# Cross attention with layer norm on one core: the key sums are moved into the attention visit, and five smaller moves

## What is computed

```python
q = (x @ Wq.T + bq), k = (ctx @ Wk.T + bk), v = (ctx @ Wv.T + bv)     # split into 16 heads of 32
att = softmax(q @ k.T / sqrt(32))                                     # over the 750 keys
out = x + ((att @ v) @ Wo.T + bo)
out = (out - mean) / sqrt(var + 1e-5) * gamma + beta                  # over the 512 features
```

## Time and profile before

| | |
|---|---|
| median of 3 runs | 644.46 us (643.81 to 645.33) |
| the profiled execution | 644.03 us, of which the span of the instructions is 642.0 us |
| granted TensorE clock, mean | 0.996 |
| busy: TensorE, VectorE, ScalarE, GpSimd | 617.8, 480.1, 350.5, 453.5 us |

### The profile page before, as it was taken

The page is one execution under the profiler, slowest core; times in us unless marked ns, Lnnn a source line. Parts: engine busy times, 40 slices in busy tenths (PEclk is TensorE's granted clock), DMA queues, the critical chain, the costliest instruction groups (busy, mean ns, idle before and its releaser), DMA issues.

```text
span 642.0 us, 13640 instructions
## 1 busy us (share of the span) xinstructions
PE 617.8 (96%) x5217; PEld 422.1 (66%) x5217; DVE 480.1 (75%) x680; ACT 350.5 (55%) x673; POOL 453.5 (71%) x443
## 2 busy tenths in 40 slices
PE   9989999999999999999999999999999999999994
PEld 7756676766666667766666666666677666665542
DVE  4677677777887688776887678876888788765895
ACT  4524566565565456564665655654565656443661
POOL 9401686975878588785879858785887878866853
PEclk9999999999999999999999999999999999999998
DMA  9367633663256613754137631566136431330011
GB/s 298 127 180 166 148 85 73 125 149 67 63 112 140 147 42 89 162 138 107 28 87 162 146 77 47 128 148 143 35 89 165 99 66 40 96 91 21 2 50 37
DMA packets 96016, 67.02 MB, mean 104 GB/s; under 512 B 69892, under 2 KB 82192, under 8 KB 95952
## 3 DMA queue, kind: packets, MB, share of 16 engines
q1 hardware_dynamic: 95952, 66.16, 41.9%
HBM read 24.52 MB, written 3.67 MB: 44 GB/s over the span
## 4 chain that ended last, share of the span: by engine, by line
PE 81%; DVE 15%; issue 2%; ACT 1%; POOL 0%; POOLq 0%; DVEq 0%
PE ps_task L595 36%; PE ps_task L646 11%; PE ps_scores L606 11%; PE ps_scoresT L630 10%; DVE top L912 6%; PE ps_task L554 4%; PE ps_task L672 2%; PE ps_scores L595 2%; DVE attn_sums L919 2%; DVE attn_parts L934 2%; DVE y L881 1%; DVE stats L884 1%; DVE parts L869 1%; PE ps_scores L574 1%; PE ps_scores L658 1%
## 5 line engine op out<-in xcount | busy, mean ns | idle before, releaser
L793 ACT ACTIVATE probsT<-ps_scoresT 125x448 f32<-125x448 f32 x384 | 203.8, 545 | 200.6 <-PE ps_scoresT L630 198.9
L912 DVE TENSOR_REDUCE top<-ps_scores 112x1 f32<-112x750 f32 x256 | 235.4, 927 | 78.8 <-PE ps_scores L606 77.8
L1020 POOL TENSOR_TENSOR pair_sums<-probsT 125x672 f32<-125x672 f32 x122 | 198.5, 1627 | 111.0 <-ACT probsT L793 101.8
L630 PE MATMUL ps_scoresT<-stacks 100*125 100x224 f16 x768 | 134.8, 260 | 1.7 <-ACT probsT L793 1.1
L595 PE MATMUL ps_task<-wvT,ctxT 128*125 128x512 f16 x564 | 134.9, 379 | 0.9 <-DVE parts L869 0.9
L595 PE MATMUL ps_task<-ctxT,wkT 128*128 128x375 f16 x708 | 130.7, 323 | 0.1
L606 PE MATMUL ps_scores<-stacks 96*112 96x512 f16 (+1 forms) x512 | 126.2, 328 | 2.5 <-DVE top L912 2.5
L630 PEld LDWEIGHTS ps_scoresT<-stacks 100*125 100x125 f16 x768 | 93.6, 137 | 40.9 <-ACT probsT L793 6.4
L1025 POOL TENSOR_TENSOR head_sums<-pair_sums 125x224 f32<-125x224 f32 x122 | 88.8, 728 | 11.4
L595 PEld LDWEIGHTS ps_task<-wvT,ctxT 128*125 128x125 f16 x564 | 73.2, 136 | 33.7 <-DVE parts L869 1.1
L1028 POOL TENSOR_TENSOR head_sums<-head_sums,pair_sums 125x224 f32<-125x224 f32 x122 | 87.1, 714 | 9.6
(11 more groups left out here) (100 smaller groups left out, 524.1 us busy)
## 6 DMA issues: line engine op xcount, KB each, us to landing
stacks<-parts SPq DMA_DIRECT2D x256, 60.9 KB, 2.0
ctx_in<-in_ctx SPq DMA_DIRECT2D x8, 768.0 KB, 5.6
stacks<-parts SPq DMA_DIRECT2D x128, 46.9 KB, 2.0
resid<-in_x SPq DMA_DIRECT2D x8, 448.0 KB, 4.2
ctx_in<-in_ctx SPq DMA_DIRECT2D x7, 512.0 KB
out_y<-y SPq DMA_DIRECT2D x16, 224.0 KB, 2.4
x_in<-in_x SPq DMA_DIRECT2D x8, 256.0 KB, 3.1
stacks<-parts SPq DMA_DIRECT2D x128, 14.0 KB, 1.8
```

Of the source, the lines that this page charges most:

```text
L630: last = nc.tensor.matmul(ps_scoresT[0:KP, piece % 2, NQ * i:NQ * i + NQ], stacks[:, g, h, KP * k:KP * k + KP], stacks[:, g, h, Qc], start ...
L793: nc.scalar.activation(probsT[0:KP, g % 2, h, 2 * j:2 * j + 2, :].rearrange("p k q -> p (k q)"), ps_scoresT[0:KP, piece % 2, 0:2 * NQ], AC ...
L912: nc.vector.tensor_reduce(top[0:QP, g % 2, HG * q + h:HG * q + h + 1], ps_scores[0:QP, s % RING, 0:NK], AX.X, ALU.max).then_inc(top_ready, 1)
L1020: nc.gpsimd.tensor_tensor(pair_sums[0:KP], probsT[0:KP, g % 2, h, 0:3, :], probsT[0:KP, g % 2, h, 3:6, :], ALU.add).then_inc(pair_sums_rea ...
```

## The change

- `sum_keys` goes into step 1, right behind `attend`; `copy_attn` goes from step 3 to step 2. The steps of the inversion and all that follows stay.
- The pair sums of each unit's fourth head (h = 3, `FOURTH`) are made on VectorE (`add_fourth`, one addition of three tiles to three, 125 by 672) in step 0 of the unit, behind `save_task`; GpSimd waits for them and does the other two additions. The buffer `pair_sums` stays one for both engines, so `add_fourth` waits until GpSimd has finished the third head.
- The tasks ("V", 4) and ("Q", 3) change places (steps 7 and 8). ("V", 2) goes from step 28 to 24, ("Q", 0) from 24 to 26, ("Q", 1) from 26 to 28.
- `rstd_of` on GpSimd goes from steps 20 and 22 to 21 and 23, `times_gamma` on VectorE from 26 and 29 to 24 and 25, `plus_beta` on GpSimd from 27 and 30 to 24 and 26.
- ("V", 2) and the last three tiles of Wo leave the prologue; iteration 0 does them in steps 1, 9, 18 and 20. The load of Wo is split in halves; the second goes into `y`.
- The first `fill_stack(1)` is issued by GpSimd; `load_ctx(1, 0)` is issued before the first `fill_stack(0)`.

```diff
+    WO_HALF = DT // 2
-    OWN = {0: ("K", 2, 1), 2: ("Q", 2), 4: ("K", 3, 1), 5: ("V", 3), 7: ("V", 4), 8: ("Q", 3), 10: ("V", 5)}
-    NEXT = {12: ("K", 0, 0), 13: ("K", 1, 0), 15: ("V", 0), 16: ("V", 1), 21: ("K", 0, 1), 23: ("K", 1, 1), 24: ("Q", 0),
-            26: ("Q", 1), 28: ("V", 2), 29: ("K", 2, 0), 31: ("K", 3, 0)}
+    OWN = {0: ("K", 2, 1), 2: ("Q", 2), 4: ("K", 3, 1), 5: ("V", 3), 7: ("Q", 3), 8: ("V", 4), 10: ("V", 5)}
+    NEXT = {12: ("K", 0, 0), 13: ("K", 1, 0), 15: ("V", 0), 16: ("V", 1), 21: ("K", 0, 1), 23: ("K", 1, 1), 24: ("V", 2),
+            26: ("Q", 0), 28: ("Q", 1), 29: ("K", 2, 0), 31: ("K", 3, 0)}
+    FIRST = {1: ("V", 2), 9: ("W", "o", 1), 18: ("W", "o", 2), 20: ("W", "o", 3)}
-    SUMS_BEHIND = 2
-    STAGES = {**{("attend", k): (2, VISIT) for k in range(KT)}, "sum_keys": (2, SUMS_BEHIND), "copy": (2, 3), ("invert", 0): (2, 4),
+    STAGES = {**{("attend", k): (2, VISIT) for k in range(KT)}, "sum_keys": (2, VISIT), "copy": (2, 2), ("invert", 0): (2, 4),
               ("invert", 1): (2, 4), "scale": (2, 5), "high": (2, 6), "low": (2, 7)}
+    FOURTH = HG - 1
-    GAMMA_STEPS = (3 * UNIT + 2, 3 * UNIT + 5)
+    RSTD_STEPS = (2 * UNIT + 5, 2 * UNIT + 7)
+    GAMMA_STEPS = (3 * UNIT, 3 * UNIT + 1)
+    BETA_STEPS = (3 * UNIT, 3 * UNIT + 2)
...
-            load_w("o", Wo)
+            load_wo_half(0)
+            sp.wait_ge(bias_turned, 1)
+            load_wo_half(1)
             sp.wait_ge(task_saved, prologue.index(("Q", 0)) + 1)
-            fill_stack(0)
             load_ctx(1, 0)
+            fill_stack(sp, 0, stacked[0])
             load_x(1)
...
-            sp.wait_ge(task_saved, prologue.index(("Q", 1)) + 1)
-            fill_stack(1)
             load_resid(0)
...
-                    if s % UNIT != SUMS_BEHIND:
-                        for u, g_u in due("sum_keys", b, s):
-                            sum_keys(u, g_u)
+                    for u, g_u in due("sum_keys", b, s):
+                        sum_keys(u, g_u)
...
-                    if s % UNIT == SUMS_BEHIND:
-                        for u, g_u in due("sum_keys", b, s):
-                            sum_keys(u, g_u)
...
+            def add_fourth(u, g):
+
+                dve.wait_ge(probs_ready, PIECES * (u + 1))
+                dve.wait_ge(head_sums_ready, sums_on_gpsimd(HG * u + FOURTH))
+                nc.vector.tensor_tensor(pair_sums[0:KP], probsT[0:KP, g % 2, FOURTH, 0:3, :], probsT[0:KP, g % 2, FOURTH, 3:6, :],
+                                        ALU.add).then_inc(fourth_sums_ready, 1)
...
                         if u is not None and s % UNIT == i and vector_sums(HG * u + h):
                             sum_head(u, (g - back) % UNITS, h)
+                        elif u is not None and s % UNIT == i and h == FOURTH and not is_last(u):
+                            add_fourth(u, (g - back) % UNITS)
...
+            pool.wait_ge(task_saved, prologue.index(("Q", 1)) + 1)
+            fill_stack(pool, 1, stacked_by_pool)
             pool.wait_ge(rows_loaded, 3 * DMA)
...
-                            if s == O_STEPS[q] + 2:
+                            if s == RSTD_STEPS[q]:
                                 rstd_of(q, b - 1)
                         for q in range(2):
-                            if s == GAMMA_STEPS[q] + 1 and not (isinstance(b, int) and b == B):
+                            if s == BETA_STEPS[q] and not (isinstance(b, int) and b == B):
                                 plus_beta(q, b - 1)
```

More of the change, by code:

```diff
@@ L477, in after @@
                     return before + max(tasks[STEP_OF[t]][1] for t in kinds) + 1
+                moved_readers = max((place + 1 for s, (t, place, _) in tasks.items() if isinstance(b, int) and b == 0 and s in FIRST and t[0] == "V"), default=0)
                 def wait_split(t):
@@ L484, in turn_when_free @@
                 def turn_when_free(t):
-                    sp.wait_ge(task_ready, after(LAST_READERS[t]) if t in LAST_READERS else before)
+                    sp.wait_ge(task_ready, after(LAST_READERS[t]) if t in LAST_READERS else before + moved_readers)
                     sp.sem_inc(split_seen, 1)
@@ L570, in task @@
                 elif kind == "W":
-                    if t[1] == "k" or t[2] == 0:
+                    if t[1] == "o":
+                        pe.wait_ge(wo_loaded[t[2] // WO_HALF], DMA)
+                    elif t[1] == "k" or t[2] == 0:
                         pe.wait_ge(w_loaded[t[1]][t[2]], DMA)
+                    for piece in inside:
+                        scores_keymajor(*piece)
+                    rows_in = wo_in[t[2] // WO_HALF][:, t[2] % WO_HALF] if t[1] == "o" else w_in[:, "qkv".index(t[1]), t[2]]
                     for k in range(DT):
-                        last = nc.tensor.transpose(bank[:, P * k:P * k + P], w_in[:, "qkvo".index(t[1]), t[2], P * k:P * k + P], ident[:])
+                        last = nc.tensor.transpose(bank[:, P * k:P * k + P], rows_in[:, P * k:P * k + P], ident[:])
                 elif kind == "O":
@@ L602, in scores @@
                 if q == 0:
-                    pe.wait_ge(stacked[g][h], DMA * STACK_DMAS * (batch + 1))
+                    if g != 1:
+                        pe.wait_ge(stacked[g][h], DMA * STACK_DMAS * (batch + 1))
+                    elif isinstance(batch, int) and batch == 0:
+                        pe.wait_ge(stacked_by_pool[h], DMA * STACK_DMAS)
+                    else:
+                        pe.wait_ge(stacked[g][h], DMA * STACK_DMAS * batch)
                 need(pe, top_ready, STEPS * batch + s - RING + 1)
```

63 lines of the change are left out of this document (38 added, 25 removed), and 7 rows, old and new, of the table prologue.

## The result

The changed kernel takes 649.06 us (median of 6 executions, 647.55 to 652.66), the kernel before 644.43 in the same comparison. The ratio is 1.0074, 95% interval 1.0058 to 1.0090: slower by 0.7%, where the forecast was 641.0 and faster. The profiled execution of the changed kernel took 647.55 us, with a span of 644.7.

The account below looks back on a forecast made before the run. TensorE, busy in 96% of the span, was taken as the bound; -5.9 - 4.5 + 0.9 - 2.5 + 8.5 = -3.5 us against the profiled 644.03 gave 640.5, as median 641.0; range 632 to 650.

Parts of the forecast that it names:

- Sums, -5.9: Key sums on TensorE: eight matmuls cost 0.61 us alone, 0.40 inside the visit; 0.21 gained in 28 units, -5.9 us.
- Rival C: Key sums inside the visit save nothing, the cost being the same in any place: 646.9 us, chance 0.1.
- the visits of steps 9 and 17 have more [cover] (a long task stands before them): Fourth head's addition stays hidden in these visits, with more than the 0.7 us of cover at step 25; cost nothing.
- Rival B: TensorE waits in the visits of steps 25 and 1 for the fourth head, if add_fourth ends after 239.65: 652, chance 0.15.
- Wait before step 25, -4.5: TensorE's wait for K 1 1's save goes, since V 2 in step 24 is longer than Q 0: 5 x 0.89 us.
- Context load, +8.5: Late load delays ScalarE's cast; TensorE stands 1.7 us in steps 10 and 12 of iterations 2 to 6: +8.5 us.
- Rival A: The context load causes no wait, and the terms without it hold: 632.4 us, chance 0.25.
- SP is late by 6.15 us: SP's queue, from fill_stack(0) on, starts that much later against the visit, because Q 0 is saved later.
- Iteration 6, +0.9: Without V 2 there, the visit of step 25 waits for the same save with nothing to fill step 24: +0.9 us.
- at most +1.15: Upper bound of iteration 6's loss at the visit of step 25: 1.15 us of Q 0 is done behind it.
- Prologue, -2.5: V 2 and three tiles of Wo leave the prologue (-3.9 us) and partly come back in iteration 0: net -2.5 us.
- GpSimd's 16 transfers: Unit 1's stack issued by GpSimd at the start costs nothing, up to about 2.2 us for each issue.

Follow-up runs that it names:

- e12: The kernel before with only the pair sum of each unit's fourth head moved to VectorE: 647.39 us, ratio 1.006 to the kernel before.
- e13: e12 with the key sums moved into the visit and the copy to step 2 as well: 648.52 us, ratio 1.008 to the kernel before.
- e5: e1 with rstd, gamma and beta also back in their old steps: 643.97 us, ratio 0.999 to the kernel before.
- e1: The changed kernel with Q 0, Q 1 and V 2 back in steps 24, 26 and 28: 638.48 us, ratio 0.990 to the kernel before.
- e11: The kernel before with only rstd one step later, in steps 21 and 23: 637.71 us, ratio 0.990 to the kernel before.
- e14: e5 with the fourth head's pair sum on GpSimd again from unit 29 on: 642.50 us, ratio 0.996 to the kernel before.
- e2: The changed kernel with the load of the context's second half issued ahead of the transposes of tiles 0 and 1: 641.53 us, ratio 0.995 to the kernel before.
- e4: The changed kernel with Q 0 in step 23, V 2 in 24, K 1 1 in 26, Q 1 in 28: 640.62 us, ratio 0.993 to the kernel before.
- e10: e5 with the fourth head's pair sum on GpSimd again for units 30 and 31 alone: 644.77 us, ratio 1.001 to the kernel before.
- e6: e1 with the fourth head's pair sum made by GpSimd again (no add_fourth): 654.61 us, ratio 1.017 to the kernel before.

## Why the prediction was wrong

Five runs lead from the kernel before to the changed one, each with one more part of the change. By their medians: the fourth head on VectorE +3.0 us (e12), the sums in the visit +1.1 (e13, which the spread of these two runs does not tell from nothing), the shorter prologue with the exchange of V 4 and Q 3 and the other issues at the start -4.6 (e5), rstd, gamma and beta -5.5 (e1), the places of the three tasks +10.6 (the changed kernel). That is the measured +4.6. The parts inside the -4.6 were not run alone; 2.7 of it stand at the first scores in the traces. Of the -5.5, rstd alone gives -6.7 on the kernel before (e11).

- **Sums, -5.9.** The size was right: 0.22 to 0.23 us for each unit (e5, e13), 28 units. Rival C falls. What failed is "the visits of steps 9 and 17 have more [cover] (a long task stands before them)": in iteration 6 step 17 has no such task, and the 2.6 us (4.3 with the clock in e13) eat most of the gain. The cover was checked in a full batch only. Rival B had the mechanism and the point from which it decides, but its two steps were 25 and 1 of full batches, which held, but for 0.4 us once.
- **Wait before step 25, -4.5.** The size was right and it did go in iterations 1 to 5, but the step that named its cause failed. I took K 1 1's save as late because Q 0 is a short task. It was late because L934 ahead of it ran beside a pair sum of GpSimd (e11). A sign of it lay in the earlier trace rows, L934's longest of 1955 ns against a median of 451, which I used to bound the fourth head only (the six ahead of these waits take 1.47 us each, the longest stands in the last unit). So the new order was credited with 4.5 us that rstd brings alone, and could bring nothing: e1, without it, has no such wait.
- **Context load, +8.5.** Right in mechanism and chain, line by line; the term was mis-sized a little. SP was 6.7 us behind the visit (predicted 6.8), the load was issued 34.2 us behind it (33.2) and landed after 6.0 (5.6). Against e1, steps 8 to 15 of iterations 1 to 6 lose 0.11, 0.85, 1.68, 0.87, 1.54 and 2.15: 7.2 us. Iteration 6 has the largest stall and not the mean: its load is issued 5.4 us behind the scores of step 8, those of iterations 2 to 5 4.3 to 4.8. Why was not tried. Rival A falls.
- **What else hangs on SP's late start.** The step "SP is late by 6.15 us" was followed only to the context load. The very first transfers of that queue are wanted by step 0 of the next batch; TensorE waits 3.7 us for them, in four batches (2.8 of them up to 480 us). The four issues and the landing (4.5 us) had to be set against the 4.0 us from the queue's start to step 0, and were not.
- **Iteration 6, +0.9.** It cost 5.3 us: load 1.9, sums in step 17 2.7, and 0.9 in steps 24 to 31. For the visit of step 25 the term was right: without V 2 it waits for K 1 1's save, where e1 has no wait.

```profile
534.12 2.48 PE L670 MATMUL ps_task<-probsT,v 125*32 125x224 f32 x48 [1.03 <-DVE parts L890]
```

  The bound "at most +1.15" looked at this one visit, while the load and the sums had their own worst case there.
- **Last unit of iteration 7, no term.** +3.2 us. VectorE is full there, steps have no task, so TensorE is fed maximum by maximum, and an instruction ahead of a maximum can delay it. "VectorE was idle for over a microsecond in each visit" is not true of these steps. e12 and e14 show that the fourth head of step 24 is enough for such a loss; in the changed kernel the two gamma steps stand there too, and I did not part them.
- **Prologue, -2.5**: measured 2.97 at the first step and 2.91 at the second batch, of which the first two units' sums are 0.4; so the size was right. **GpSimd's 16 transfers**: hidden, as said, at 0.50 to 0.74 us an issue.

The sum missed by 7.0 us in the profiled execution (640.5 against 647.55). The step starts place 6.9 of it, with each term taken where it was forecast. The start and iterations 0 and 1 came as forecast, to 0.1 us. Iterations 2 to 5 miss by +1.6: the stack costs 2.8 there, the load 1.9 less than forecast (4 x 1.7 = 6.8, measured 4.9), and 0.7 is in small pieces, most of it in steps 0 to 7 of iteration 2. Iteration 6 misses by +3.5, of which 2.9 in steps 16 to 23. Iteration 7 misses by +1.8: 3.2 in the last unit, less 1.4 in steps 0 to 7. There the kernel before has a wait of 1.1 us in the visit of step 1 for VectorE's save, which is gone in the changed kernel and in e1. e11 still has it and e5 has one of 1.9, so rstd alone does not take it away, and the new steps of gamma and beta have a part in it: a gain of the change that no term had.

## What to carry to other kernels

A term that holds for the steady batch has to be tried again in the iterations that lack work (the last ones): covers are made of tasks, and there the tasks are missing while the moved instruction is not. When a task is moved, write down every reader of the queue behind it, the nearest first, not only the one that looks critical. And before an order is changed to remove a wait, look at the instruction that is late and at those ahead of it, and compare their durations with the medians of their lines: a stretched one can point to a neighbour on another engine. Here moving that neighbour by one step brought 6.7 us (e11).

## What the runs showed of the hardware

- VectorE's L934, with two SBUF operands, takes 0.44 us, and 1.47 when it starts 0.39 us behind a pair sum of GpSimd. In six batches of the kernel before TensorE waited 0.8 us for the save behind it.
- A hole of TensorE can cost a second time: its granted clock falls to 0.50 behind it in some executions and stays at 1.00 in others. The same wait of 2.6 us in iteration 6 is followed by 0.50 in the traces of e1, e2, e4, e10, e13 and e14, and by 1.00 in those of the changed kernel and e5. The trace of e6 has six waits of 1.9 us for the sums, and three of them are followed by 0.50. That this makes the spread of a kernel's times is argued from e14, whose executions part by their mean clock.
- SP's issue of a small transfer takes 0.59 us (median), and at times more, up to 1.7 in the kernel before and 2.1 in the changed one. What stretches it was not tried.
- Of the 16 transfers that GpSimd issues, the eight of this form landed 2.5 us (median, 2.0 to 4.6) behind their issue, SP's of the same form 2.0; an issue takes GpSimd 0.50 us, the first 0.74. Columns: transfers, KB, median us to landing.

```profile
stacks<-parts SPq DMA_DIRECT2D x248, 60.9 KB, 2.0
...
stacks<-parts POOLq DMA_DIRECT2D x8, 60.9 KB, 2.5
```

The Trainium skill (DMA: Bandwidth & Descriptors, Specifications) gives about 0.6 us from SyncE and about 1 us from GpSimd to the first byte, a difference of 0.4; the medians here differ by 0.5, which eight transfers of such a spread do not settle.
